# Position-bias loop: the third layer of the max kind directly behind that of the relu kind

## The reference

```python
pos = grid_q[:, :, None, :] - grid_kv[:, None, :, :]
bias = jnp.sign(pos) * jnp.log1p(jnp.abs(pos))
bias = jax.nn.relu(bias @ cpb_w1 + cpb_b1)          # 2 -> 32
bias = jax.nn.relu(bias @ cpb_w2 + cpb_b2)          # 32 -> 32
bias = (bias @ cpb_w3 + cpb_b3).reshape(b, GROUPS, H * W, Hd * Wd)   # 32 -> 1
sim = jnp.einsum('bhid,bhjd->bhij', qh, kh) + bias
```

## Time and profile before

| | |
|---|---|
| median of 3 runs | 1708.6 us (1703.53 to 1709.87) |
| the profiled execution | 1709.64 us |
| its span | 1707.9 us |
| mean granted clock of TensorE | 0.946 |
| busy in the span: PE / DVE / ACT / POOL | 1503.9 / 883.2 / 855.8 / 321.0 us |
| cycle 0's first block of line 673 | 91.92 us |
| cycle 63's first block | 438.45 us |

### The profile page before, as it was taken

How to read it: one execution, slowest core, us unless ns; L and a number is a source line. 1 busy time by engine, 2 the same in 40 slices (tenths; PEclk the granted TensorE clock), 3 DMA queues, 4 the chain that set the end, 5 groups by cost and what they waited for, 6 DMA issues and landing times. The chain is left out here.

```text
span 1707.9 us, 29513 instructions
## 1 busy us (share of the span) xinstructions
PE 1503.9 (88%) x12320; PEld 740.2 (43%) x12320; DVE 883.2 (52%) x1348; ACT 855.8 (50%) x1164; POOL 321.0 (19%) x139
## 2 busy tenths in 40 slices
PE   6989999999777987999999998899999999638778
PEld 4322222222343765656666665554444444316333
DVE  2478888888753535677676776110001000248343
ACT  3467777777443445677777765322222222150441
POOL 0646666666220001000000000000000000020000
PEclk8589999999998998899999999899999999879889
DMA  1000000000020004244443440000000000000000
GB/s 63 1 2 2 2 2 2 2 2 2 2 81 16 1 1 172 106 155 173 150 154 130 173 172 2 1 1 0 1 0 0 0 0 0 30 0 3 2 1 25
DMA packets 21087, 69.63 MB, mean 41 GB/s; under 512 B 736, under 2 KB 17248, under 8 KB 18656
## 3 DMA queue, kind: packets, MB, share of 16 engines
q1 hardware_dynamic: 20672, 66.76, 10.5%
q10 hardware_dynamic: 288, 1.05, 0.2%
HBM read 33.21 MB, written 34.60 MB: 40 GB/s over the span
## 5 line engine op out<-in xcount | busy, mean ns | idle before, releaser
L553 POOL TENSOR_TENSOR l_work<-l_a_scores,l_work 128x2048 f32<-128x2048 f32 x64 | 233.0, 3641 | 128.7 <-PE banks L673 128.7
L1867 PE MATMUL banks<-s_h,pack_l2f_l3f 128*128 128x512 f32 x512 | 221.0, 592 | 0.0
L1894 ACT ACTIVATE s_h<-banks,pack_l2f_l3f 128x512 f32<-128x512 f32 x128 | 88.0, 687 | 241.2 <-PE banks L1867 175.8
L613 DVE TENSOR_TENSOR l_work<-banks,sc_negc 128x1024 f32<-128x1024 f32 x128 | 156.1, 1220 | 49.2 <-PE banks L720 33.0
L573 ACT ACTIVATE l_work<-banks,pack_l 128x1024 f32<-128x1024 f32 x128 | 142.7, 1114 | 75.5 <-PE banks L673 74.7
L673 PE MATMUL banks<-l_work,pack_l 32*32 32x512 f32 x4096 | 159.1, 603 | 23.7 <-ACT l_work L573 19.9
L1457 PE MATMUL banks<-pack_l2a,r_e 128*128 128x128 f32 x1024 | 144.7, 285 | 26.0 <-ACT r_e L1509 26.0
L1509 ACT ACTIVATE r_e<-banks,r_max 128x1024 f32<-128x1024 f32 x128 | 142.6, 1114 | 44.6 <-DVE r_max L1550 44.6
L1544 DVE TENSOR_REDUCE r_raw<-banks 128x1 f32<-128x640 f32 (+1 forms) x128 | 109.5, 855 | 106.1 <-PE banks L1438 106.1
L1867 PEld LDWEIGHTS banks<-s_h,pack_l2f_l3f 128*128 128x128 f32 x512 | 97.3, 190 | 122.5 <-issue 122.5
L1438 PE MATMUL banks<-r_k,r_q 32*128 32x128 f32 (+3 forms) x832 | 148.8, 466 | 1.1 <-DVE r_v L1382 1.1
(11 more groups left out here) (387 smaller groups left out, 2132.5 us busy)
## 6 DMA issues: line engine op xcount, KB each, us to landing
distances<-r_rd SPq DMA_DIRECT2D x16, 2048.0 KB, 6.3
r_band<-distances SPq DMA_DIRECT2D x16, 1536.0 KB, 7.0
pack_l2f_l3f<-pack_dram_l2f SPq DMA_DIRECT2D x1, 2244.5 KB, 10.3
pack_l2f_l3f<-pack_dram_l3f SPq DMA_DIRECT2D x1, 1248.5 KB, 5.6
residual<-x ACTq DMA_DIRECT2D x2, 512.0 KB, 6.0
out<-residual SPq DMA_DIRECT2D x4, 256.0 KB, 2.0
pack_l<-pack_dram_l SPq DMA_DIRECT2D x1, 945.0 KB, 7.3
pack_l2a<-pack_dram_l2a SPq DMA_DIRECT2D x1, 715.0 KB, 5.4
```

Of the source, the lines that this page charges most:

```text
L553: pool.tensor_tensor(image(H1R[:, (c + 1) % 3]), bc(a, 2, 16), bc(b, 3, HW), ALU.add).then_inc(sem("added"), 1)
L613: dve.tensor_tensor(image(H2M[:, (2 * c + part) % 3]), image(PS[:, MAX + j:MAX + j + 2]), bc(NEGC[:, j:j + 2, n, i, rows(half)], 3, HW), A ...
L1867: ins = pe.matmul(bank, W["w2"][:, col:col + P], H1[:, c, m], start=(m == 0), stop=(m == HB - 1))
L1894: act.activation(H[:, c, k], PS[:, g % 8], ACT.Tanh, bias=bias).then_inc(sem("tanh"), 1)
```

## The change

`layer3_max(c - 1)` is called right behind `layer3_relu(c - 1)`, between the two parts of layer 2, and no longer at the end of the cycle. The two calls after the loop, for cycle 63, stand as they were. The other engines' programs are the same.

```diff
             if c % 4 == 3 and c + 1 < CYCLES:
                 negb((c + 1) // 4)
             if c:
                 layer3_relu(c - 1)
+                layer3_max(c - 1)
             layer2_relu(c, 1)
             layer2_max(c, 1)
-            if c:
-                layer3_max(c - 1)
         layer3_relu(CYCLES - 1)
         layer3_max(CYCLES - 1)
```

## The result

| | before | changed |
|---|---|---|
| median (4 runs each) | 1707.78 us (1703.53 to 1709.87) | 1753.59 us (1750.47 to 1754.42) |
| ratio | | 1.0268, 95% interval 1.0244 to 1.0292 |
| profiled execution, its span | 1709.64, 1707.9 us | 1753.88, 1752.1 us |

The kernel is slower by 45.8 us, by the spans by 44.2. The forecast was 1747 us with a range of 1735 to 1761.

The account below looks back on a forecast made before the run. Two round trips per cycle, matmul to ScalarE eviction to matmul, were taken to bound the loop. 21.7 + 12.9 + 2.1 + 1.3 = +38.0 us on a median of 1708.6 gave 1747 us, range 1735 to 1761.

Parts of the forecast that it names:

- the second gap: PE's time from layer 2's second block to the next cycle's first block, 2.46 us before the change, filled by layer3_max.
- Step 1: Plain cycles: both layer 3 groups between layer 2's two blocks delay the second, 5.51 us for 4.81, +21.7 us in all.
- Block 2: The second run of layer2_relu and layer2_max in a cycle, 16 matmuls, writing the same two banks as the first.
- T+3.06: 3.06 us after T, the start of the cycle's first layer 2 block; the second block's forecast start, 2.35 before.
- Step 2: From layer 2's second block to the next cycle's first stays 2.45 us, PE idling about 1.3 us; nothing regained.
- The rival of a shorter trip: A layer 2 block directly following another on the same tiles saves 0.12 to 0.15 us per cycle: 1738 us, chance 0.08.
- Step 3: Cycles with negb: PE already bound the time between layer 2's blocks, so +0.86 us each, 15 times, +12.9 us.
- Step 4: Cycles with query_keys: L701 no longer waits for tile_out, so 6.53 us against 6.39, 15 times +0.14, +2.1 us.
- Step 5: The loop's ends: cycle 1 +0.9 us, cycle 63 with its last L720 +0.4 us, together +1.3 us.
- Step 6: Waits on max2, VectorE and POOL's add: the earlier layer3_max brings no new wait, cost nothing.
- the signs of being right: Plain cycles 5.5 us, PE's wait on L573 1.3 us, no L701 wait on L620, granted clock 1.00, later stages equally long.
- a rival of 0.04: The granted clock falls to half in the loop for a third of the cycles: 42 us more, 1789 us, chance 0.04.

Follow-up runs that it names:

- evict_half: The changed kernel with relu2 evicting only the first 256 of 512 columns of each bank: 1728.95 us, ratio 1.0151.
- the filler: The changed kernel with four more matmuls of layer3_max's shape behind part 1 in 63 cycles, results unused: 1743.89 us, beside the changed kernel again 1742.76 us.
- m3_negb_cycles: The kernel before with layer3_max moved ahead of part 1 only in cycles with c % 4 == 3, 15 with negb and cycle 63: 1718.35 us, ratio 1.0077.

## Why the prediction was right

- **What bounds the loop.** Two round trips through the banks of the relu kind. Shown by `evict_half` for the second gap (0.42 us shorter eviction, 0.42 shorter gap) and by the filler (a group more, no time more).
- **Step 1, the first gap overflows.** Block 2 at T+3.06 forecast, 3.05 measured. The unknown price, L711 until L720, was taken as 0.86 between bounds of 0.84 and 1.00, and is 0.88. L720 until block 2, taken as 1.00, is 0.97, so two small errors cancel in 3.06. The row of L654 came nearer than the row with a change of tiles, but with some luck: it was read as if all of it ran at a granted clock of 0.50, and over the whole group the clock was 0.54 (window below, columns as in rows 2), so that 0.84 was too low a bound.

```profile
87.36:90.71 3.35, 3.35 (x32) 1.67 (x32) 0.00 (x0) 3.35 (x4) 0.00 (x0) 0.54 0.00 0
```

- **Step 2, the second gap is empty.** 2.45 forecast, 2.46 measured, PE idle 1.30 of it. The rival of a shorter trip found nothing: a block behind a block starts its eviction 1.18 us in, as before.
- **Step 3, `negb`.** +0.86 a cycle measured in twelve of the fifteen, and in `m3_negb_cycles` in all.
- **Step 4, `query_keys`.** The changed kernel's L620 ends at 298.54, 1.07 us into a cycle that began at 297.47, as worked out from VectorE's order. That cycle took 6.60 us (304.07 - 297.47), forecast 6.53: L701 starts 1.23 us in and L711 1.06 behind it, where I had 1.20 and 1.02.
- **Step 5, ends.** The last L720 starts 6.30 us into cycle 63 (488.98 - 482.68), forecast 6.28. At the other end cycle 2 starts 1.2 us later (108.45 for 107.25), and that this is near the 0.9 that I had counted for cycle 1 is luck. PE comes to the loop 2.0 us later (93.91 for 91.92), with nothing changed ahead of it. Cycle 1 then holds L720's 0.88 us more, as forecast, but takes 7.0 us where it took 7.8, because L701 and L711 ran at the half clock there before and run at the full one now: 1.06 and 0.88 us to the next group for 1.86 and 1.83. Below are L701 and a window around it, of the kernel before and then of the changed one:

```profile
101.10 1.93 PE L701 MATMUL banks<-l_q,l_km 128*128 128x512 f32 x2
101.00:104.00 3.00, 3.00 (x18) 0.56 (x10) 2.88 (x3) 1.80 (x2) 0.87 (x1) 0.55 0.00 0
```

```profile
103.09 1.13 PE L701 MATMUL banks<-l_q,l_km 128*128 128x512 f32 x2
102.00:105.00 3.00, 3.00 (x42) 0.77 (x30) 2.88 (x4) 2.43 (x3) 1.88 (x1) 1.00 0.00 0
```

- **Step 6, no new waits, and the other engines' slack.** No wait of L720's matmuls on L613 is in the changed kernel's list, and L567 waits 9.6 us on POOL where it waited 9.8.

**What was mis-sized** is the clock. The sum put it at nothing, and a granted clock of 1.00 was among the signs of being right; the forecast had a fall only as a rival of 0.04 that would cost 42 us over a third of the cycles, an all-or-nothing reading of the rows. It came in three short drops, 5.2 us, and these are most of what the sum of 38.0 lacks of the 44.2 between the spans. Further, 0.6 us more than forecast are in the plain cycles, 0.4 in those with `query_keys`, 0.2 in the other cycles with `negb`, and 0.3 before cycle 2. With these the last L720 comes 44.6 us later (488.98 for 444.37), and what follows it is 0.4 us shorter than before, as good as unchanged, as forecast.

## What to carry to other kernels

A wait of 0.3 us before each step, in a loop where three engines are 78 to 91% busy, can be the visible rest of a round trip that other work nearly fills. Before moving a group of matmuls, write down for each gap how long the trip is and how much of it PE already works: a group that leaves a gap which the trip keeps open gives nothing back, and one that joins another gap costs what doesn't fit there. Here, of 0.88 us, that was 0.70 in a plain cycle, and about all of it in one with `negb`, whose gap was full. And look for the gain such a move brings elsewhere, here L701's 10 us: it may be had by another engine's order at no price.

## What the runs showed of the hardware

- Two groups of four float32 matmuls with 512 columns on 128x32 tiles, back to back, start 0.88 us apart at the full clock. From such a group to one on 32x32 tiles it is 0.97 to 1.00. So a change of tile shape costs about 0.1 us here, the difference. The Trainium skill, "TensorEngine Tiling (Array Packing)", section "Tiling Modes", says that it drains TensorE and gives no figure; the traces agree with it, and show why it didn't matter: the changed kernel makes two changes fewer in each cycle and is slower.
- From cycle 2 on, the granted clock dropped to half for some microseconds two or three times per execution in the changed kernel, where PE is busy 79% of the loop, once with the shorter eviction in it (83%), four times with both groups in the second gap (79%), and never in the loops of the kernel before (91%) or with the filler (95%, two executions). It also never did in the two kernels with the move in a quarter of the cycles (90 and 87%). Each drop in the changed kernel fell into a cycle with `negb` and cost 1.6 to 1.8 us; the four with both groups in the second gap fell into plain cycles. That more idle time of PE in every cycle brings the drops is what these runs suggest, the filler's above all; what exactly starts one, they don't show.
